# Relative and causal attention of a post-norm transformer kernel: the loops over steps written out on every engine

## The chip, the cores and the metric

One core of one Trainium2 chip runs the whole program, all nine stages in one launch. The metric is device time in microseconds (us) of one execution. The engines have their own instruction streams and meet at semaphores: TensorE (PE; PEld is its weight load), VectorE (DVE), ScalarE (ACT), GpSimd (POOL) and SyncE (SP, which issues most DMAs).

## The reference

The input is x of 8 batches x 512 tokens x 128 features. Four blocks follow one another, each with a residual and a layer norm: a one-head attention, a causal attention with 16 heads of 8 features together with a top-2-of-8 experts layer, an attention with relative positions, and a low-rank feed-forward. The change concerns two of the stages:

```python
# causal attention (16 heads of 8), b = 8, t = 512
scores = jnp.einsum('bqhd,bkhd->bhqk', q, k)
scores = jnp.where(mask, -jnp.inf, scores)
attn = jax.nn.softmax(scores / np.sqrt(HEAD_DIM), axis=-1)
ctx = jnp.einsum('bhqk,bkhd->bqhd', attn, v).reshape(b, t, EMB)
...
# relative attention (16 heads of 8)
AC = jnp.einsum('bhid,bhjd->bhij', q + u_bias[None, :, None, :], k)
BD = jnp.einsum('bhid,hjd->bhij', q + v_bias[None, :, None, :], rp)
BD = _rel_shift(BD)
attn = jax.nn.softmax((AC + BD) * scale, axis=-1)
out = jnp.einsum('bhij,bhjd->bhid', attn, v)
```

## The kernel before

Nothing is left to a scheduler: each phase writes out by hand what every engine does, in which order, and which semaphore count it waits for. Names of tiles in the profile begin with the phase's letter: `c_` for `phase_causal`, `r_` for `phase_relative`.

Both attention phases cut their work into NI = 32 steps: a step is one group of 4 heads (G = 4, NG = 4 groups) of one batch (NB = 8).

Causal, a step n: PE makes the row scores (L757, and the mask from `halves`, L765) three steps ahead in `ps_rows`, DVE takes their maxima (L917, L923), PE turns the maxima (L776), DVE splits them (L937, L939), and SP copies them beside the queries (L701). PE makes the scores of the step itself the other way round in `ps_keys` (L786), ACT takes the exponential (L860), POOL clears what lies above the diagonal (L891), PE sums probabilities and values (L798) in `ps_out`, ACT copies that to `osb` (L867; once a step) and SP stores it (L722). POOL issues the loads of step n + 5 (L691, L694).

Relative, a step n is 16 tiles u (four heads, four blocks of 128 queries each). For each tile PE makes one content matmul two tiles ahead in `ps_ac` (L1955), turns the finished scores of this tile in `ps_keys` (four transposes, L1962), and writes one bank of position scores of step n + 2 in `ps_wide` (short matmuls on 32 rows of weights, L1946, 192 in a step); after every fourth tile it sums a head in `ps_out` (L1973). DVE adds content and position and takes the maximum (L2078) and subtracts it (L2086). ACT takes the exponential (L2044), copies each bank to `wide` (L2023), and sends `wide`, 2,224 KB for half a step, to HBM (L2028); SP fetches it back skewed, 2,048 KB (L1866), which is the shift of the reference. SP also loads queries, keys and values (L1852, L1854, L1859) and stores the sums (L1894). ACT copies `ps_out` to `osb` once a step (L2034).

What the change touches is `steps` in each of the two phases (L704 and L1834): it calls an engine's `step` for every n. In the causal phase a loop on the engine (`Fori`, L705) runs 3 times over a body of 8 steps, and the last 8 are written out. In the relative phase the first 4 steps are written out, a loop (L1838) runs 6 times over a body of 4 steps, and the last 4 are written out. In a loop's body the count `it` is a register: waits compare a semaphore with a value worked out in registers, and DMAs take their places in HBM from registers. In the steps written out all of these are constants. `left` tells a step how many steps follow it, as far as it needs to know.

Each engine calls `steps` after its own preparation, so each of them has a loop of its own (POOL only in the causal phase).

Of the kernel before, what the change touches and what calls it, by code (L numbers as in the profile page):

```python
# [14 lines left out]
NB = 8  # L15
# [6 lines left out]
NI = NB * NG  # L22
# [18 lines left out]
class Chain:  # L41
# [6 lines left out]
    def step(self, ins):  # L48
        self.k += 1
        ins.then_inc(self.sem, 1)  # L50
        self.eng.wait_ge(self.sem, self.n * self.per + self.k)
# [563 lines left out]
def phase_causal(nc, sems, qk_stacks, v9_in, mask_in, ident_in, ctx_out):  # L615
# [14 lines left out]
    SLOTS = 8  # L630
    AHEAD = 3
    FIRST = 5
    ROUNDS = NI // SLOTS
# [7 lines left out]
    with ExitStack() as ctx:  # L641
# [60 lines left out]
                        .then_inc(m_loaded[s], 16)  # L702

        def steps(step, eng):  # L704
            with eng.Fori(0, ROUNDS - 1) as it:  # L705
                for s in range(SLOTS):
                    step(it, s, SLOTS)
            for s in range(SLOTS):
                step(ROUNDS - 1, s, SLOTS - 1 - s)

        @block.sync
        def _(sp):
# [21 lines left out]
            for n in range(2):  # L734
                sp.wait_ge(m_split, n + 1)
                load_maxima(sp, n)
            steps(step, sp)
            for s in range(SLOTS):
                sp.wait_ge(loaded[s], LOADS * ROUNDS)
# [5 lines left out]
        def _(pe):  # L745
# [103 lines left out]
            for f in range(BANKS):  # L849
                key_tiles(0, 0, 0, f)  # L850
            steps(step, pe)

        @block.scalar
        def _(act):
            def exponentials(n, p, f):
                e, c = FILLS[f]
                width = sum(WIDTH[j] for j in KEYS[c])
                at = OFF[KEYS[c][0]]
                act.wait_ge(keys_ps, NF * (2 * n + p) + f + 1)
                act.activation(probs[:, p, e, at:at + width], ps_keys[f % BANKS][:, 0:width], ACT.Exp, scale=SCALE)\  # L860
                    .then_inc(exp_done, 1)

            def take(n, s, uses):

                act.wait_ge(pair_done, 2 * n + 4)
                act.wait_ge(stored[s % 2], STORES * (uses + 2))
                act.activation(osb[:, s % 2, :, :, :].rearrange("q p e i -> q (p e i)"), ps_out[:, :], ACT.Copy)\  # L867
                    .then_inc(out_sb, 1)

            def step(it, s, left):  # L870
                n = SLOTS * it + s
                for p in range(2):
                    act.wait_ge(pair_done, 2 * n + p + 1)
                    for f in range(NF):
                        exponentials(n, p, f)
                        if p == 0 and f == 1:
                            take(n - 1, s - 1, SLOTS // 2 * it + (s - 1) // 2)

            act.sem_inc(exp_done, BANKS)
            steps(step, act)  # L880
            take(NI - 1, SLOTS - 1, NI // 2 - 1)
# [890 lines left out]
def phase_relative(nc, sems, qu_stacks, qv_stacks, k_stacks, v9_in, r_stack, ident_in, skew_dram, ctx_out):  # L1772
# [9 lines left out]
    STEP = 4  # L1782
# [3 lines left out]
    with ExitStack() as ctx:  # L1786
# [46 lines left out]

        def steps(step, eng):  # L1834

            for j in range(STEP):
                step(0, j, j == 0, 4)
            with eng.Fori(1, NB - 1) as it:  # L1838
                for j in range(STEP):
                    step(it, j, False, 4)  # L1840
            for j in range(STEP):
                step(NB - 1, j, False, STEP - 1 - j)

        def uses(it, j):

# [3 lines left out]
        def _(sp):  # L1849
# [61 lines left out]
            sp.wait_ge(wide_ps, 4 * NBK)  # L1911
            load_queries(0, 3)
            steps(step, sp)
            store(NI - 1)
            for s in range(2):
# [9 lines left out]
        def _(pe):  # L1925
# [87 lines left out]
            content_tile(0, 0, 0)  # L2013
            content_tile(0, 0, 1)
            steps(step, pe)
            value_head(NI - 1, 1, G - 1)

        @block.scalar
        def _(act):
# [40 lines left out]
            for n in range(2):  # L2060
                for c in range(2):
                    for bk in range(NBK):
                        copy_wide(n, n, c, bk)
                    send(n, n, c)
            steps(step, act)
            take_sums(NI - 1)

# [136 lines left out]
```

## Time and profile before

| what | us |
| --- | --- |
| three timed runs | 2204.28, 2189.57, 2207.71 (median 2204.28) |
| the profiled execution's own time | 2203.24 |
| its span, first to last instruction | 2201.5 |
| around the span | 1.7 |
| causal phase, first to last copy at L867 | 322.2 to 622.1 |
| relative phase, first to last copy at L2034 | 1212.2 to 2074.7 |

Times in the profile are microseconds from the start of the span. PE's busy time comes from pipelined matmuls with modelled ends. PEclk is the share of TensorE's full clock that was granted. "issue" as what ended an idle time means that the profile shows nothing that the engine waited for. A sequencer's own instructions (branch, register arithmetic) carry a q behind the engine's name.

### The profile page before, as it was taken

To read this page: it belongs to the slowest core of one execution; us is meant where nothing else is said; L and a number is where in the kernel's file an instruction comes from. 1 tells how busy PE (TensorE), PEld (TensorE's weight loads), DVE (VectorE), ACT (ScalarE), POOL (GpSimd) and SP (SyncE) were. 2 spreads that over 40 slices of the span, in tenths; PEclk is the share of its full clock that TensorE was granted. 3 is DMA by queue.
4 is the path that set the end of the run, shared out by engine and by line. 5 is a ranking of instruction groups with operands and counts; after the bars stand their busy time and mean duration, and the time that the engine had idled before them with its cause. 6 is when DMAs were issued, how large, how long until landed. Compare 5 with 4: busy or idle time off the path is not lost. (4 is left out here: it accounts for less than half of the span.)

```text
span 2201.5 us, 53937 instructions
## 1 busy us (share of the span) xinstructions
PE 1600.2 (73%) x19079; PEld 991.7 (45%) x19079; DVE 1297.3 (59%) x3126; ACT 1055.4 (48%) x2028; POOL 343.9 (16%) x659
## 2 busy tenths in 40 slices
PE   5532447777754999996536998687879787899647
PEld 2211214444433666663223555454546454555423
DVE  4774277667635666764314766474657565667636
ACT  4332316656722333222325766465657565667333
POOL 2232325545441000001300000000000000000023
PEclk8766659989966999998757988797989898889869
DMA  1114722222144121212889999898999999899621
GB/s 38 43 40 140 236 58 63 60 55 62 38 131 155 65 84 53 105 54 81 267 226 332 373 344 345 296 342 284 348 338 341 351 323 352 274 346 350 193 83 57
DMA packets 190973, 425.29 MB, mean 193 GB/s; under 512 B 37328, under 2 KB 86384, under 8 KB 181328
## 3 DMA queue, kind: packets, MB, share of 16 engines
q1 hardware_dynamic: 167776, 242.57, 35.5%
q10 hardware_dynamic: 12240, 150.28, 16.8%
q0 software_dynamic: 10720, 29.11, 5.1%
q8 instruction: 170, 2.79, 0.5%
q14 instruction: 67, 0.55, 0.1%
HBM read 218.59 MB, written 203.03 MB: 192 GB/s over the span
## 5 line engine op out<-in xcount | busy, mean ns | idle before, releaser
L2078 DVE CUSTOM_DVE_ANT_0 r_shifted<-r_ps_ac,r_shifted 128x512 f32<-128x512 f32 x512 | 351.9, 687 | 343.5 <-PE r_ps_ac L1955 327.0
L2044 ACT ACTIVATE r_probs<-r_ps_keys 128x512 f32<-128x512 f32 x512 | 309.7, 605 | 275.0 <-PE r_ps_keys L1962 249.5
L2023 ACT ACTIVATE r_wide<-r_ps_wide 128x512 f32<-128x512 f32 (+1 forms) x576 | 329.8, 590 | 102.1 <-PE r_ps_wide L1946 101.2
L1962 PE MATMUL r_ps_keys<-r_ident,r_shifted 128*128 128x128 f32 x2048 | 334.1, 288 | 7.5 <-issue 5.5
L1962 PEld LDWEIGHTS r_ps_keys<-r_ident,r_shifted 128*128 128x128 f32 x2048 | 273.8, 149 | 56.4 <-issue 15.4
L1946 PE MATMUL r_ps_wide<-r_r,r_qv 48*32 48x96 bf16 (+12 forms) x6144 | 238.3, 257 | 77.3 <-issue 67.2
L2086 DVE TENSOR_SCALAR r_shifted<-r_shifted,r_mx 128x512 f32<-128x512 f32 x512 | 249.2, 487 | 18.3
L1955 PE MATMUL r_ps_ac<-r_k,r_qu 128*128 128x512 bf16 x512 | 211.7, 414 | 60.8 <-DMA r_v<-v 32.8
L860 ACT ACTIVATE c_probs<-c_ps_keys 128x512 f32<-128x512 f32 (+1 forms) x384 | 174.8, 530 | 154.6 <-PE c_ps_keys L786 154.5
L1946 PEld LDWEIGHTS r_ps_wide<-r_r,r_qv 48*32 48x32 bf16 x6144 | 103.6, 95 | 179.0 <-issue 177.1
L1422 ACT ACTIVATE e_silu<-e_ps_a 128x1024 f32<-128x1024 f32 x64 | 65.7, 1027 | 216.1 <-PE e_ps_a L1355 215.9
L1973 PE MATMUL r_ps_out<-r_probs,r_v 128*9 128x128 f32 x4096 | 150.0, 285 | 21.6 <-issue 20.9
L923 DVE TENSOR_REDUCE c_mx_off<-c_ps_rows 128x2 f32<-128x768 f32 (+2 forms) x192 | 120.8, 686 | 68.3 <-PE c_ps_rows L757 68.3
L1069 POOL MEMSET n_zeros<- 128x4 f32 x1 | 0.1, 101 | 967.0 <-POOLq L1786 967.0
L1495 DVE TENSOR_TENSOR e_gu<-e_silu,e_ps_b 128x1024 f32<-128x1024 f32 x64 | 78.2, 1221 | 93.8 <-PE e_ps_b L1355 93.8
L1355 PE MATMUL e_ps_a<-e_hT_half,e_w_half 128*128 128x512 f32 x384 | 125.7, 463 | 4.3 <-DVE e_w_half L1550 4.3
L1973 PEld LDWEIGHTS r_ps_out<-r_probs,r_v 128*9 128x9 f32 x4096 | 103.2, 93 | 49.8 <-issue 36.1
L891 POOL TENSOR_SCALAR_AFFINE_SELECT c_probs<-c_probs 128x256 f32<-128x256 f32 x256 | 98.0, 407 | 162.3 <-ACT c_probs L860 161.8
L1955 PEld LDWEIGHTS r_ps_ac<-r_k,r_qu 128*128 128x128 bf16 x512 | 49.4, 97 | 163.7 <-issue 129.2
L1370 PE MATMUL e_ps_o<-e_weighed,e_w 128*128 128x512 f32 x256 | 120.5, 594 | 0.0
L786 PE MATMUL c_ps_keys<-c_qk 50*128 50x512 bf16 (+3 forms) x512 | 95.8, 317 | 27.7 <-ACT c_probs L860 19.5
L757 PE MATMUL c_ps_rows<-c_qk 48*128 48x128 bf16 (+2 forms) x896 | 78.0, 261 | 50.9 <-DVE c_mx_off L923 41.6
(214 smaller groups left out, 2157.0 us busy)
## 6 DMA issues: line engine op xcount, KB each, us to landing
skew<-r_wide ACTq DMA_DIRECT2D x64, 2224.0 KB, 11.8
r_shifted<-skew SPq DMA_DIRECT2D x64, 2048.0 KB, 18.0
e_weight_all<-weights SPq DMA_DIRECT2D x8, 2048.0 KB, 7.4
c_qk<-qk_stacks POOLq DMA_DIRECT2D x64, 192.0 KB, 3.7
stack<-d_part SPq DMA_DIRECT2D x96, 128.0 KB, 2.7
qk_stacks<-b_part SPq DMA_DIRECT2D x48, 128.0 KB, 3.6
qk_stacks<-b_part POOLq DMA_DIRECT2D x48, 128.0 KB, 3.7
stack<-d_part POOLq DMA_DIRECT2D x48, 128.0 KB, 3.7
```

The costliest lines, as they stand in the source:

```text
L860: act.activation(probs[:, p, e, at:at + width], ps_keys[f % BANKS][:, 0:width], ACT.Exp, scale=SCALE)\
L923: last = dve.tensor_reduce(off[:, :, NT * p + b], ps[:, :, at:at + width], AX_X, ALU.max)
L1355: last = pe.matmul(ps[:, k, :], w[a][:, e, k * P:(k + 1) * P], hT_halves[b][:, s, :], start=(i == 0), stop=(i == 2))
L1370: last = pe.matmul(ps_o[s][:, :], w3[:, e, k * P:(k + 1) * P], weighed[:, e % 4, k, :], start=(e == 0 and k == 0), stop=(e == NE - 1 and k ...
L1946: last = pe.matmul(ps[Q * a:Q * a + Q, frm - lo:to - lo], qv[rows, h, q0 + one:q0 + one + Q], r[rows, g // 2, h, at:at + to - frm], start= ...
L1955: pe.matmul(ps_ac[u % 2][:, :], qu[:, s, h, b * P:(b + 1) * P], k[:, s, h, :], start=True, stop=True)\
L1962: last = pe.transpose(ps_keys[u % 2][:, j * P:(j + 1) * P], shifted[:, s, u, j * P:(j + 1) * P], ident[:, :])
L1973: last = pe.matmul(ps_out[Q * b:Q * b + VW, h * P:(h + 1) * P], v9[:, s, j, h * VW:(h + 1) * VW], probs[:, h % 2, j, b * P:(b + 1) * P], s ...
L2023: act.activation(wide[:, s, c, lo:hi], ps_wide[bk % BANKS][:, 0:hi - lo], ACT.Copy).then_inc(wide_sb, 1)
L2044: act.activation(probs[:, h % 2, :, b * P:(b + 1) * P], ps_keys[u % 2][:, :].rearrange("p (j i) -> p j i", j=NT), ACT.Exp, scale=SCALE).th ...
L2078: dve.tensor_tensor_reduce(out=shifted[:, s, u, :], in0=ps_ac[u % 2][:, :], in1=shifted[:, s, u, :], scale=1.0, scalar=LOWEST, op0=ALU.add ...
L2086: dve.tensor_scalar(shifted[:, s, u, :], shifted[:, s, u, :], mx[:, u:u + 1], None, ALU.subtract).then_inc(s_ready, 1)
```

## The change

Both `steps` become one loop in the program that writes the kernel, so each engine gets 32 steps one behind the other, with constants in every wait and every address, and with neither loop nor branch. `left` is cut at the largest value that a step looks for (8, and 4). What a step does and in which order is the same.

```diff
@@ phase_causal
         def steps(step, eng):
-            with eng.Fori(0, ROUNDS - 1) as it:
-                for s in range(SLOTS):
-                    step(it, s, SLOTS)
-            for s in range(SLOTS):
-                step(ROUNDS - 1, s, SLOTS - 1 - s)
+            for n in range(NI):
+                step(n // SLOTS, n % SLOTS, min(SLOTS, NI - 1 - n))
@@ phase_relative
         def steps(step, eng):
 
-            for j in range(STEP):
-                step(0, j, j == 0, 4)
-            with eng.Fori(1, NB - 1) as it:
-                for j in range(STEP):
-                    step(it, j, False, 4)
-            for j in range(STEP):
-                step(NB - 1, j, False, STEP - 1 - j)
+            for n in range(NI):
+                step(n // STEP, n % STEP, n == 0, min(4, NI - 1 - n))
```

On PE in the causal phase, the end of the loop's body before (ISA and REGISTER_ALU are register work; the branch goes back to the first keys matmul of the next 8 steps):

```order
L786 MATMUL c_ps_keys<-c_qk 128x512
L783 REGISTER_ALU
L786 MATMUL c_ps_keys<-c_qk 128x384
L786 MATMUL c_ps_keys<-c_qk 128x128
L832 ISA
L798 MATMUL c_ps_out<-c_probs,c_v 9x128 x20
L705 REGISTER_ALU
L705 COMPARE_AND_BRANCH
```

On PE in the causal phase, the same place now (L795 is the old L798, L783 the old L786, L754 the old L757):

```order
L783 MATMUL c_ps_keys<-c_qk 128x512 x2
L783 MATMUL c_ps_keys<-c_qk 128x384
L783 MATMUL c_ps_keys<-c_qk 128x128
L795 MATMUL c_ps_out<-c_probs,c_v 9x128 x20
L783 MATMUL c_ps_keys<-c_qk 128x384
L783 MATMUL c_ps_keys<-c_qk 128x128
L754 MATMUL c_ps_rows<-c_qk 128x384 x2
```

The branch and the register work between the matmuls are gone; the matmuls stand in the same order.

On PE in the relative phase, the end of the loop's body and, behind the branch, what follows it:

```order
L1946 MATMUL r_ps_wide<-r_r,r_qv 32x224
L1946 MATMUL r_ps_wide<-r_r,r_qv 32x32
L1838 REGISTER_ALU
L1838 COMPARE_AND_BRANCH
L1955 MATMUL r_ps_ac<-r_k,r_qu 128x512
L1962 MATMUL r_ps_keys<-r_ident,r_shifted 128x128 x4
```

On PE in the relative phase, the first tile of the loop's body before:

```order
L1838 ISA
L1955 MATMUL r_ps_ac<-r_k,r_qu 128x512
L1959 REGISTER_ALU
L1962 MATMUL r_ps_keys<-r_ident,r_shifted 128x128 x4
L1991 ISA
L1931 ISA
L1946 MATMUL r_ps_wide<-r_r,r_qv 32x32
```

On PE in the relative phase, a tile now (L1947 is the old L1955, L1954 the old L1962, L1938 the old L1946, L1965 the old L1973):

```order
L1965 MATMUL r_ps_out<-r_probs,r_v 9x128 x16
L1947 MATMUL r_ps_ac<-r_k,r_qu 128x512
L1954 MATMUL r_ps_keys<-r_ident,r_shifted 128x128 x4
L1938 MATMUL r_ps_wide<-r_r,r_qv 32x160
L1938 MATMUL r_ps_wide<-r_r,r_qv 32x128
```

No matmul changed its place; what stood between them for the registers is gone on every engine.

## Rows read from the trace of the kernel before

**Rows 1.** The page: span, PE's busy share, DMA busy in 40 slices.
```profile
span 2201.5 us, 53937 instructions
PE 1600.2 (73%) x19079; PEld 991.7 (45%) x19079; DVE 1297.3 (59%) x3126; ACT 1055.4 (48%) x2028; POOL 343.9 (16%) x659
DMA  1114722222144121212889999898999999899621
```

**Rows 2.** The copies that mark a step (duration ns min/median/max, first and last start).
```profile
L867 ACT ACTIVATE c_osb<-c_ps_out x33: 597/597/603, 322.2 to 622.1; 128x512 f32<-128x512 f32 x33
...
L2034 ACT ACTIVATE r_osb<-r_ps_out x32: 591/603/604, 1212.2 to 2074.7; 128x512 f32<-128x512 f32 x32
```

**Rows 3.** Causal windows: length, busy us of PE, PEld, DVE, ACT, POOL; PEclk, DMA share, GB/s.
```profile
394.00:408.70 14.70, 8.96 (x137) 5.45 (x139) 6.68 (x11) 6.12 (x13) 5.05 (x12) 0.77 0.18 41
408.70:460.80 52.10, 40.77 (x802) 25.57 (x800) 40.10 (x66) 35.63 (x78) 29.84 (x67) 1.00 0.27 65
469.60:497.40 27.80, 20.92 (x268) 11.52 (x270) 13.45 (x22) 12.15 (x27) 9.99 (x23) 0.63 0.18 42
533.60:585.90 52.30, 40.76 (x800) 25.76 (x798) 40.11 (x66) 35.65 (x79) 27.79 (x64) 1.00 0.25 56
```

**Rows 4.** Relative windows, same columns; steps between copies: 3, 3, 4, 4, 4, 21.
```profile
1212.20:1289.20 77.00, 71.06 (x1202) 45.38 (x1201) 54.46 (x145) 54.83 (x107) 0.00 (x0) 0.93 1.03 357
1289.20:1371.70 82.50, 73.83 (x1205) 46.76 (x1208) 54.50 (x145) 55.22 (x107) 0.00 (x0) 0.90 1.00 354
1415.20:1534.60 119.40, 95.78 (x1605) 61.13 (x1604) 72.83 (x193) 73.19 (x142) 0.00 (x0) 0.89 0.92 321
1647.80:1760.20 112.40, 94.20 (x1604) 60.42 (x1603) 72.60 (x194) 73.08 (x142) 0.00 (x0) 0.91 0.96 341
1879.90:1988.20 108.30, 97.21 (x1602) 61.73 (x1600) 72.65 (x194) 73.12 (x142) 0.00 (x0) 0.89 0.97 333
...
1371.70:1988.20 616.50, 505.21 (x8401) 321.92 (x8400) 381.32 (x1009) 383.90 (x737) 0.00 (x0) 0.88 0.94 328
```

**Rows 5.** The loops' branches (duration ns min/median/max, first and last start).
```profile
L1838 PEldq COMPARE_BRANCH  x6: 76/5835/6406, 1395.9 to 1981.8; - x6
...
L705 PEldq COMPARE_BRANCH  x3: 79/4432/4572, 393.1 to 550.2; - x3
...
L1838 DVEq COMPARE_BRANCH  x6: 55/63/68, 1386.1 to 1972.3; - x6
```

**Rows 6.** PE's timeline behind the first and the fifth jump back, relative phase.
```profile
1402.45 0.61 PE L1955 MATMUL r_ps_ac<-r_k,r_qu 128*128 128x512 bf16 x1 [5.82 <-issue]
...
1408.47 0.63 PE L1946 MATMUL r_ps_wide<-r_r,r_qv 48*32 48x32 bf16 x8 [4.56 <-issue]
...
1867.96 0.61 PE L1955 MATMUL r_ps_ac<-r_k,r_qu 128*128 128x512 bf16 x1 [5.67 <-issue]
...
1873.71 0.62 PE L1946 MATMUL r_ps_wide<-r_r,r_qv 48*32 48x32 bf16 x8 [4.29 <-issue]
```

**Rows 7.** Windows around the first jump back, columns as in rows 3.
```profile
1395.00:1407.50 12.50, 3.09 (x29) 1.91 (x27) 2.37 (x6) 2.17 (x5) 0.00 (x0) 0.50 1.02 382
1407.50:1420.00 12.50, 11.53 (x171) 7.02 (x172) 6.43 (x17) 6.68 (x13) 0.00 (x0) 0.74 0.34 68
```

**Rows 8.** DMA between 1371.7 and 1988.2: all packets, and the instruction queue's packets.
```profile
DMA packets 72714, 201.98 MB, mean 328 GB/s; under 512 B 14206, under 2 KB 21304, under 8 KB 67273
...
q8 instruction: 83, 1.36, 0.9%
```

**Rows 9.** PE's register arithmetic for two waits (duration ns min/median/max).
```profile
L1931 PEldq ALU_OP  x384: 32/32/36, 1285.0 to 1980.3; - x192
...
L783 PEldq ALU_OP  x237: 32/32/36, 322.2 to 549.0; - x119
```

**Rows 10.** PE's timeline: two idle times away from a branch, relative phase.
```profile
1228.86 0.61 PE L1973 MATMUL r_ps_out<-r_probs,r_v 128*9 128x128 f32 x11 [1.70 <-issue]
...
1452.85 0.28 PE L1946 MATMUL r_ps_wide<-r_r,r_qv 48*32 48x256 bf16 x1 [2.28 <-issue]
```

## The prediction

> **What bounds the kernel now.** I read the page first, for the stages in which the two loops run: PE is busy 73% of the 2201.5 us span, and the DMA engines stand at 8 or 9 tenths in the second half, where the relative phase lies [rows 1]. Then I looked for a mark that comes once a step, and took ACT's copy of the sums: 33 in the causal phase, 32 in the relative one [rows 2]. Cutting the trace at these copies shows the pace.
>
> In the causal phase six steps take 52.1 us, 8.7 us each, with the clock at full and no engine above 80%: PE, DVE and ACT hand work to each other (40.8, 40.1 and 35.6 us busy of 52.1). After eight and after sixteen steps, where the loop jumps back, the pace breaks: the step at 394.0 takes 14.7 us, the two at 469.6 take 27.8 us [rows 3].
>
> In the relative phase the six steps 1212.2 to 1371.7 take 77.0 + 82.5 = 159.5 us, 26.6 each, with DMA at its limit (share 1.00 to 1.03, 354 to 357 GB/s). Of these, three are written out and three lie in the loop's first pass, and no jump back lies between. Four steps of the last pass, again without one, take 108.3 us. Four steps with one jump back take 119.4 us, at best 112.4. Over the 21 steps from 1371.7 to 1988.2, which hold all five jumps back, the pace is 616.5 / 21 = 29.4 us, and the DMA share sinks to 0.94 [rows 4]. So this phase is bound by the DMA round trip of the wide scores, except behind a jump, where PE holds everybody up.
>
> The branch rows say whose jump it is. PE's compare-and-branch takes 76 ns once in the relative phase (the exit, which falls through) and up to 6406 ns otherwise, median 5835; in the causal phase 79 ns once, and 4432 and 4572 ns. DVE's takes 55 to 68 ns [rows 5]. PE's timeline has the cost in two parts: 5.82 us idle before the first content matmul of the new pass, then one tile, then 4.56 us idle before the first wide matmul, both ended by "issue", at the first jump; 5.67 and 4.29 us at the fifth [rows 6]. 
>
> Two jumps back in the causal phase go. The step at 394.0 falls from 14.7 to 8.7 us, the two at 469.6 from 27.8 to 2 x 8.7 = 17.4: 6.0 + 10.4 = 16.4 us. The branches alone are 4.57 + 4.43 = 9.0 of that. The rest is what follows: the granted clock is 0.77 and 0.63 in these windows and 1.00 in the steady ones, so part of the matmuls there ran at 1.2 instead of 2.4 GHz behind PE's idle time [rows 3, 5]. What is late next is the old round of PE, DVE and ACT at 8.7 us. Bounds for the term: 9 and 16.4; I take 16.4, since the windows on either side of the jumps keep to 8.7.
>
> Five jumps back in the relative phase go. Counted at PE they are 5 x (5.75 + 4.4) = 51 us, with the means of the first and the fifth [rows 6]. But PE is not alone on the path, so I count by pace as well. While PE stood at the first jump, the DMA engines still worked off what was queued (share 1.02, 382 GB/s from 1395.0 to 1407.5) and ran dry only then (0.34, 68 GB/s in the next 12.5 us) [rows 7]: PE's stall becomes a hole in the DMA stream, a little later and about as long, 0.66 x 12.5 = 8.3 us. Ten steps without a jump take 159.5 + 108.3 = 267.8 us, 26.8 each; 21 such steps take 562.4 us instead of 616.5. That is 54.1 us, and the term that I take. What is late next is the DMA traffic. It bounds the gain: 201.98 MB in these 21 steps [rows 8] at 382 GB/s need 529 us, so no more than 87 us. From below, four steps keep 108.3 us of their last pass, 27.1 each: 616.5 - 569 = 47 us.
>
> The register arithmetic goes, at 32 ns each on PE: 384 for the wide banks alone, 237 for the key tiles [rows 9]. I put it at nothing. The cover is in the trace: six looped causal steps take 52.1 us and six written-out ones 52.3 [rows 3]. In the relative phase the DMA engines cover it. If that cover were thin, 384 x 32 ns = 12 us is the end on the side of a gain; none is on the side of a loss, as nothing is added in its place.
>
> The DMAs' addresses become constants on SP and POOL. Their queues run ahead of the data and the bytes are the same, so I put this at nothing too, bounded by the same two causal windows, in which SP stores and POOL loads with registers in one and constants in the other.
>
> The loops' set-up and the exits (76 and 79 ns on PE) are worth less than 1 us together.
>
> Code grows, which costs if it has to be fetched more often. PE's was fetched all along: the instruction queue moved 83 packets in these 21 steps [rows 8], four a step, so a pass of four steps was loaded anew each time. The number stays or falls. Crossing into a new piece of code can show: PE idles 2.28 us before the wide matmul at 1452.85 inside the loop, and 1.70 us at 1228.86 in steps already written out, both with "issue" [rows 10]. Such idle times are in the 26.8 us already.
>
> The sum: 2203.24 - 16.4 - 54.1 - 0 = 2132.7 us, against the profiled execution, which lies 1.0 under the median of 2204.28. I predict 2132.
>
> At the branch two pages can be weighed against the rows. The Trainium skill, "Advanced Engine Details and Errata", section Control Flow Timing, gives a compare-and-branch about 108 ns; by that, an estimate from this page, the seven jumps back cost 0.8 us in all and the change would be worth nothing. The Trainium skill, "Runtime: NRT & Kernel Launch", section Instruction fetch mechanics, says that a taken branch to code outside the two blocks at hand has to wait for a DMA fetch. This trace sides with the second for PE (4.4 to 6.4 us) and with the first for DVE (63 ns).
>
> **The rivals.**
>
> *The transfers hide it.* The relative phase hangs on DMA, so PE's stalls only move waiting from one place to another, and the pace stays 29.4 us. Only the causal 16.4 us are left: 2187. For it speaks the DMA share of 0.94 over the 21 steps. Against it speak the hole of 0.34 behind the jump and the windows at 26.6 and 27.1 us.
>
> *The pace goes down to the wire.* The holes left in the jump-free windows are echoes of the jumps and the start, and the phase closes up to 382 GB/s: 2203.2 - 16.4 - 87 = 2100. Against it: the first six steps, with no jump before them, had 26.6 us, and 529 / 21 would be 25.2.
>
> *A branch costs nothing; PE stood for another reason* that the rows don't name, and the time is the old one less 1 us: 2202. Against it: all seven long branches stand where a jump is taken, and both exits take under 0.1 us.
>
> *Code fetch takes the branch's place (slower).* Written out, every piece of PE's code is new, and pieces may begin at places where PE has little queued. There are 83 - 5 = 78 such crossings in the 21 steps. Two or three a pass show now, at some 2.3 us [rows 10]. From 70.5 / 2.3 = 31 more of them on the nothing is won; if the 65 or so that are hidden all showed, it is 65 x 2.3 = 150 us lost, and 2283 us. Against it: the steps 1212.2 to 1289.2, written out, kept 25.7 us each, and six written-out causal steps kept 8.7. A milder case, 15 more that show, gives 2132 + 35 = 2167, still faster.
>
> **How the numbers follow.** Chances: the forecast 0.78 (own range 2110 to 2147: 21 steps at 25.7 us, the fastest jump-free window of rows 4, or at 27.5, the slowest); down to the wire 0.08; transfers hide it 0.06; milder code fetch 0.02; branch costs nothing 0.02; code fetch slower 0.04. Range: from the wire, 2100, less the 12 us of register work at half, so 2094, up to the milder fetch with room, 2172. A measurement of this kernel tells about 1% from no change. Faster by over 1% (under 2182): 0.78 + 0.08 + 0.02 = 0.88. Within 1%: 0.06 + 0.02 = 0.08. Slower: 0.04.
>
> **What would show it.** Right: no branch rows of PE in either phase; the copies of the sums 8.7 us apart throughout the causal phase; PE without the pairs of 5 to 6 and 4 to 5 us "issue" in the relative phase; its 21 steps at 26 to 27.5 us with the DMA share at 1.0 and the granted clock above 0.90. Wrong: more "issue" idle times of 2 to 3 us on PE than two or three in four steps (code fetch); or PE idle without "issue", behind DVE or a load, and the pace near 29 (transfers). The prediction fails if the relative steps stay above 28.5 us, or if the causal saving is under 9 us.

## The result and the profile after

| | before | changed |
| --- | --- | --- |
| timed runs, median us | 2196.93 of 4 | 2139.12 of 4 (2134.5 to 2144.5) |
| the profiled execution's own time | 2203.24 | 2137.47 |
| its span | 2201.5 | 2135.9 |
| causal phase, first to last copy of the sums | 299.9 | 282.3 |
| between the phases, last causal to first relative copy | 590.1 | 595.2 |
| relative phase, first to last copy | 862.5 | 809.8 |

The ratio of the changed kernel to the one before is 0.9726, 95% interval 0.9685 to 0.9766: 2.7% faster. Between the two medians lie 57.8 us, between the two profiled executions 65.7. A second comparison, at the end, gave 0.971 (0.9671 to 0.9749).

The page of the changed kernel, the lines that answer to [rows 1], and the granted clock:

```profile
span 2135.9 us, 49719 instructions
...
PE 1582.6 (74%) x19079; PEld 983.5 (46%) x19079; DVE 1296.6 (61%) x3126; ACT 1054.0 (49%) x2028; POOL 342.4 (16%) x659
...
PEclk8765759999966999998855999899899999989869
DMA  1113822222144121121889999999999999999522
```

Every engine does the same work. 4,218 recorded instructions are gone, all of the sequencers. DMA stands at 9 tenths from the start of the relative phase nearly to its end, where it had dips before.

The windows of the changed kernel, cut at the same copies as [rows 3] and [rows 4] (columns: from:to, length, busy us of PE, PEld, DVE, ACT, POOL; PEclk, DMA share, GB/s):

```profile
393.70:402.40 8.70, 6.76 (x135) 4.31 (x133) 6.68 (x11) 5.94 (x13) 4.90 (x12) 1.00 0.29 65
402.40:454.80 52.40, 40.73 (x800) 25.84 (x798) 40.06 (x66) 35.66 (x79) 29.61 (x67) 1.00 0.27 66
463.50:480.90 17.40, 13.51 (x268) 8.59 (x266) 13.35 (x22) 11.87 (x26) 9.75 (x23) 1.00 0.28 66
1199.70:1358.20 158.50, 143.96 (x2403) 91.97 (x2401) 109.00 (x289) 109.41 (x212) 0.00 (x0) 0.90 1.03 365
1358.20:1924.90 566.70, 502.27 (x8401) 319.27 (x8400) 381.01 (x1009) 383.71 (x736) 0.00 (x0) 0.92 1.01 353
```

The causal step at the old jump takes 8.7 us instead of 14.7, the two at the second jump 17.4 instead of 27.8, and the clock is granted in full there (1.00). The register work has left nothing behind: six steps take 52.4 us as they took 52.1. In the relative phase the 21 steps of [rows 4] take 566.7 us instead of 616.5, 27.0 each, at a DMA share of 1.01 instead of 0.94.

Who waited for whom in these 21 steps, changed kernel (waiting engine and line, who released it: us in total, times, the longest):

```profile
PEld r_ps_wide L1938 <- issue: 79.5, 347, 2.6
...
PEld r_ps_ac L1947 <- DMA r_v<-v: 24.9, 7, 5.3
...
PEld r_ps_out L1965 <- issue: 19.9, 29, 2.7
...
PE r_ps_wide L1938 <- issue: 13.5, 12, 1.9
```

And the kernel before, over its 21 steps:

```profile
PEld r_ps_ac L1955 <- issue: 103.3, 241, 6.1
PEld r_ps_wide L1946 <- issue: 102.2, 342, 5.2
PE r_ps_wide L1946 <- issue: 38.5, 16, 4.8
```

The long idle times that nothing explains are gone from these steps; what is left of them is at most 2.7 us (before the sums, L1965). PE's longest single waits are now for a load, the values of the next step (up to 5.3 us, seven times), which SP issues as it does the skewed fetches. The instruction queue moved 68 packets in these steps, where [rows 8] had 83:

```profile
q8 instruction: 68, 1.11, 0.8%
```

### The profile page after: what moved, and what is told of

Same layout as the page of the kernel before. It is cut to its first block and busy times, and to the rows that moved or that the text cites. A ratio compares the mean times of both kernels' runs of the same rounds, so it can differ in the third digit from the quotient of the medians.

```text
span 2135.9 us, 49719 instructions
## 1 busy us (share of the span) xinstructions
PE 1582.6 (74%) x19079; PEld 983.5 (46%) x19079; DVE 1296.6 (61%) x3126; ACT 1054.0 (49%) x2028; POOL 342.4 (16%) x659
## 3 DMA queue, kind: packets, MB, share of 16 engines
q10 hardware_dynamic: 12240, 150.28, 17.4%
## 5 line engine op out<-in xcount | busy, mean ns | idle before, releaser
L1954 PE MATMUL r_ps_keys<-r_ident,r_shifted 128*128 128x128 f32 x2048 | 333.9, 289 | 9.9 <-issue 5.9
L1954 PEld LDWEIGHTS r_ps_keys<-r_ident,r_shifted 128*128 128x128 f32 x2048 | 272.5, 149 | 56.7 <-issue 13.9
L1938 PE MATMUL r_ps_wide<-r_r,r_qv 48*32 48x96 bf16 (+12 forms) x6144 | 237.5, 258 | 42.1 <-issue 31.1
L1947 PE MATMUL r_ps_ac<-r_k,r_qu 128*128 128x512 bf16 x512 | 210.2, 411 | 47.8 <-DMA r_v<-v 33.2
L1419 ACT ACTIVATE e_silu<-e_ps_a 128x1024 f32<-128x1024 f32 x64 | 65.7, 1027 | 216.3 <-PE e_ps_a L1352 216.3
L1938 PEld LDWEIGHTS r_ps_wide<-r_r,r_qv 48*32 48x32 bf16 x6144 | 103.6, 95 | 144.1 <-issue 142.7
L1965 PE MATMUL r_ps_out<-r_probs,r_v 128*9 128x128 f32 x4096 | 149.7, 285 | 19.4 <-issue 18.7
L1965 PEld LDWEIGHTS r_ps_out<-r_probs,r_v 128*9 128x9 f32 x4096 | 103.0, 93 | 46.6 <-issue 28.4
L1947 PEld LDWEIGHTS r_ps_ac<-r_k,r_qu 128*128 128x128 bf16 x512 | 49.3, 97 | 153.6 <-issue 76.4
L754 PE MATMUL c_ps_rows<-c_qk 48*128 48x128 bf16 (+2 forms) x896 | 75.1, 253 | 53.0 <-DVE c_mx_off L920 43.9
L783 PE MATMUL c_ps_keys<-c_qk 50*128 50x512 bf16 (+3 forms) x512 | 91.9, 309 | 20.1 <-ACT c_probs L857 19.9
```

Of the source, the lines that this page charges most:

```text
L1938: last = pe.matmul(ps[Q * a:Q * a + Q, frm - lo:to - lo], qv[rows, h, q0 + one:q0 + one + Q], r[rows, g // 2, h, at:at + to - frm], start= ...
L1947: pe.matmul(ps_ac[u % 2][:, :], qu[:, s, h, b * P:(b + 1) * P], k[:, s, h, :], start=True, stop=True)\
L1954: last = pe.transpose(ps_keys[u % 2][:, j * P:(j + 1) * P], shifted[:, s, u, j * P:(j + 1) * P], ident[:, :])
L1965: last = pe.matmul(ps_out[Q * b:Q * b + VW, h * P:(h + 1) * P], v9[:, s, j, h * VW:(h + 1) * VW], probs[:, h % 2, j, b * P:(b + 1) * P], s ...
```

## The experiments

The copies of the sums cut every trace in the same way. All causal and relative lengths below are from first to last copy, of one profiled execution each; times and ratios are of rounds against the kernel before on the same chip.

| run | causal us | between | relative us | jumps back, causal / relative | median us | ratio |
| --- | --- | --- | --- | --- | --- | --- |
| before | 299.9 | 590.1 | 862.5 | 2 / 5 | | |
| before again | 290.6 | 593.1 | 869.4 | 2 / 5 | 2204.56 | 1.0013 |
| changed | 282.3 | 595.2 | 809.8 | 0 / 0 | 2139.12 | 0.9726 |
| changed again | 281.8 | 598.3 | 809.3 | 0 / 0 | 2140.8 | 0.971 |
| causal only | 281.2 | 594.5 | 823.2 | 0 / 5 | 2157.32 | 0.9818 |
| relative only | 294.6 | 593.3 | 814.9 | 2 / 0 | 2156.9 | 0.9809 |
| PE only | 282.5 | 597.0 | 822.6 | 0 / 0 on PE | 2153.95 | 0.9779 |
| all but PE | 293.0 | 592.5 | 850.8 | 2 / 5 on PE | 2188.24 | 0.9946 |
| twelve steps | 294.7 | 591.4 | 826.3 | 2 / 1 | 2163.88 | 0.9832 |
| six steps | 308.7 | 594.2 | 844.4 | 3 / 5 | 2197.89 | 0.9994 |
| moved by 40 | 295.2 | 593.0 | 834.9 | 2 / 5 | 2177.94 | 0.989 |
| moved by 128 | 294.3 | 604.5 | 838.3 | 2 / 5 | 2192.29 | 0.997 |
| moved by 256 | 297.1 | 627.1 | 847.5 | 2 / 5 | 2224.03 | 1.0103 |
| changed, moved by 128 | 282.3 | 604.7 | 812.8 | 0 / 0 | 2146.0 | 0.9746 |

**One phase at a time.**

```diff
# phase_causal (first run) or phase_relative (second run) as in the change, the other phase as before
-            with eng.Fori(...) as it:
...
+            for n in range(NI):
```

Expected of the causal phase alone:

> Only the causal phase's loop is written out; the relative phase keeps its loop. Theory (PE's jumps back cost their own time and a stretch at the low clock): the 33 copies of the causal sums stand 8.7 us apart with no break, the causal phase ends 17 to 18 us earlier than in the kernel before, and the whole kernel is 14 to 19 us shorter (ratio 0.992 to 0.994). Rival (the gain of the whole change lies in the relative phase alone, the causal phase only moved its waiting): less than 5 us shorter.

Expected of the relative phase alone:

> Only the relative phase's loop is written out. Theory: the 21 steps between the seventh and the twenty-eighth copy of the relative sums fall from 616.5 to 562 to 570 us, no idle time of PE of 5 us and more with issue behind it at the old places, and the kernel is 43 to 55 us shorter (ratio 0.975 to 0.981). Together with the causal one alone this sums to the whole change. Rival (the transfers hide PE's jumps): under 15 us shorter.

Measured: 0.9818 (0.9768 to 0.9867) and 0.9809 (0.9769 to 0.985). The relative phase alone gives 44 us, within the 43 to 55 expected; its phase takes 814.9 us instead of 862.5. The causal phase alone gives 44 us, over twice what its theory allows. Its own part is as expected (281.2 us), but the untouched relative phase fell to 823.2 us, with its five long jumps still there:

```profile
L1835 PEldq COMPARE_BRANCH  x6: 83/5766/6542, 1381.9 to 1926.8; - x6
```

The two gains add up to 88 us, more than the change gives. So something in the relative phase's loss is not the jump: it went when code ahead of it changed its length. PE's timeline of this run behind the third jump shows one thing that is different:

```profile
1608.70 0.61 PE L1952 MATMUL r_ps_ac<-r_k,r_qu 128*128 128x512 bf16 x1 [5.89 <-issue]
1609.10 1.06 PE L1959 MATMUL r_ps_keys<-r_ident,r_shifted 128*128 128x128 f32 x4
1610.09 0.63 PE L1943 MATMUL r_ps_wide<-r_r,r_qv 48*32 48x32 bf16 x8
```

The first idle time of [rows 6] is there, 5.89 us, and the second is missing, here and behind the four other jumps: the wide matmuls follow without a pause.

**Where the code lies.** To test that, PE's code was moved without touching the loops.

```diff
# moved by 40: in phase_relative, PE, before it waits for its constants
+            for _ in range(40):
+                pe.sem_inc(bank_marks, 1)
# moved by 128 and by 256: in phase_experts, PE, before it waits for its constants
+            for _ in range(128):
+                pe.sem_inc(pads, 1)
```

> The kernel before, with 40 semaphore increments (nobody waits for them) at the start of PE's relative phase, where PE waits for its loads anyway: all of PE's code behind is moved by 40 instructions. Theory (the second idle time of 4.0 to 4.8 us after each jump is the next piece of code, which begins some 20 instructions behind the jump's target): with the target moved past that border the second idle time goes at all five jumps, and the kernel is 10 to 22 us shorter. Rival (the second idle time has to do with the start of a pass, with its first wide bank): it stays at all five, and the time is within 5 us of before.

> The kernel before with 256 semaphore increments on PE at the start of the experts phase, where PE waits for its loads anyway: PE's code behind is moved by 256 instructions, which is 16384 bytes at 64 bytes each, the size of one packet of the instruction queue. Theory (code is fetched in pieces of 16384 bytes, and the second idle time comes where a piece ends some 20 instructions behind the jump's target): the borders fall where they fell before, so the pairs of idle times are back at all five jumps and the time is that of before within 0.5%. Rival (any shift helps, or the 40 instructions of the run before acted in another way): the second idle time is gone and the kernel is 15 us or more shorter.

> The same with 128 increments, half a piece. Theory: the border lies some 150 instructions behind the jump's target, PE has queued work when it gets there, the second idle time is gone at all five jumps, and the kernel is 20 to 35 us shorter than before (ratio 0.984 to 0.991), still 15 to 30 us longer than the changed kernel, since the jumps themselves stay. Rival (the shift doesn't matter): within 5 us of before.

Moved by 40, the second idle time is gone behind all five jumps; these are the idle times behind the first and the fifth, each alone:

```profile
1405.48 0.61 PE L1955 MATMUL r_ps_ac<-r_k,r_qu 128*128 128x512 bf16 x1 [6.23 <-issue]
...
1847.70 0.61 PE L1955 MATMUL r_ps_ac<-r_k,r_qu 128*128 128x512 bf16 x1 [4.27 <-issue]
```

The relative phase falls to 834.9 us, and the kernel is 1.1% faster (0.9826 to 0.9955) for 40 instructions more, some 23 us where 10 to 22 were expected. Moved by 256, the pairs are back behind all five jumps; the first and the fifth:

```profile
1430.67 0.60 PE L1958 MATMUL r_ps_ac<-r_k,r_qu 128*128 128x512 bf16 x1 [5.30 <-issue]
1437.24 0.62 PE L1949 MATMUL r_ps_wide<-r_r,r_qv 48*32 48x32 bf16 x8 [5.11 <-issue]
...
1896.13 0.61 PE L1958 MATMUL r_ps_ac<-r_k,r_qu 128*128 128x512 bf16 x1 [5.58 <-issue]
1901.87 0.62 PE L1949 MATMUL r_ps_wide<-r_r,r_qv 48*32 48x32 bf16 x8 [4.29 <-issue]
```

Moved by 128, they are gone again and the relative phase takes 838.3 us. So the second idle time is a border between two pieces of code, 256 instructions apart, that lay just behind the jump's target.

The instruction queue's own packets say the same. Every packet of it in these traces holds 16384 bytes. Between the end of the first jump of the kernel before (1402.3) and 1406.0 the queue has no packet; then it has one, which starts at 1406.05 and takes 1.10 us (the DMA view of 1406.0 to 1408.4: packets, MB, share):

```profile
q8 instruction: 1, 0.02, 2.9%
```

PE's wide matmuls follow at 1408.47. So it goes behind all five jumps of the kernel before, of its repeat and of the kernel moved by 256: the next packet starts 3.2 to 4.6 us after the branch has ended, and PE starts again 1.2 to 1.5 us after it has landed. Moved by 40, the packet comes as late (3.4 to 4.2 us after the branch), but PE doesn't need it yet. The long branches themselves end 1.2 to 1.6 us after a packet has landed, in both phases of the kernel before and of its repeat; no packet lands within any of their short ones.

The runs with another causal phase fit too. PE's instructions ahead of the relative loop can be counted in a trace, a loop's body once. Causal only has some 4170 more than the kernel before, about 70 beyond a multiple of 256, and no second idle time. Six steps, below, has about 580 fewer: its border lies about 80 instructions behind the target instead of 16, and PE's weight load stands idle there for 1.5 to 2.4 us instead of 4.3 to 5.6. Behind its first jump:

```profile
1412.09 1.39 PEld L1973 LDWEIGHTS r_ps_out<-r_probs,r_v 128*9 128x9 f32 x28 [2.38 <-issue]
```

The times of the last two runs came out wrong against what was expected, 1.0103 and 0.997 instead of 1.00 and 0.984 to 0.991, and the table says why: the increments themselves were dear. Between the phases the run moved by 256 lost 34 to 37 us. PE's timeline at the start of the experts phase shows 50.07 us of idle time, where the kernel before had 16.36:

```profile
714.73 1.08 PE L1333 MATMUL e_ps_t<-e_ident,e_z 128*128 128x128 f32 x4 [50.07 <-issue]
```

The expectation was that PE's wait for its loads would cover them.

**The number of jumps, and a shorter body.**

```diff
# twelve steps: phase_relative, body three times as long
-            with eng.Fori(1, NB - 1) as it:
-                for j in range(STEP):
-                    step(it, j, False, 4)
+            with eng.Fori(0, 2) as half:
+                for i in range(3):
+                    for j in range(STEP):
+                        step(3 * half + i + 1, j, False, 4)
# six steps: phase_causal, SLOTS = 6 (so six buffers instead of eight), 4 passes, then 8 steps
# written out; SP's last waits count accordingly
-            with eng.Fori(0, ROUNDS - 1) as it:
+            with eng.Fori(0, 4) as it:
...
-            for s in range(SLOTS):
-                step(ROUNDS - 1, s, SLOTS - 1 - s)
+            for n in range(4 * SLOTS, NI):
+                step(n // SLOTS, n % SLOTS, min(SLOTS, NI - 1 - n))
```

> The kernel before with the relative loop's body three times as long (12 steps, 2 passes): one jump back instead of five; the causal phase as before. Theory (a price of some 10 us for each jump back): 4 x 10 = 40 us shorter, 33 to 45, and one long branch of PE left in that phase. Rival (it is not the number of jumps, but registers and loop as such): under 15 us shorter.

> The causal phase with six slots and a loop's body of 6 steps (some 1730 PE instructions instead of 2310), 4 passes and so 3 jumps back instead of 2, then 8 steps written out; the relative phase as before. Theory (a jump is dear only when its target is no longer held by PE; a body of 616 instructions elsewhere in this kernel jumps in 231 ns, one of 2310 in 4.4 us): if 1730 instructions are still held, the three branches take under 0.3 us each and the causal phase is 16 to 18 us shorter. Rival (any jump of this phase costs its 4.4 us and what follows): three breaks of 6 to 10 us instead of two, the kernel 5 to 10 us longer than before.

With one jump instead of five the relative phase takes 826.3 us, 36 us less, and the kernel is 1.7% faster (0.9768 to 0.9896). Registers and loop stayed, so it is the jumps and what comes right behind them; the pair of idle times is still there at the one that is left. The shorter body was a miss for the theory: its 1735 PE instructions (counted in the trace between two branches) are not held either.

```profile
L705 PEldq COMPARE_BRANCH  x4: 76/4573/4917, 372.5 to 555.2; - x4
```

All three jumps take 4.6 to 4.9 us, the causal phase gets longer (308.7 us, 8.9 for each jump over the 282.0 without any; the six buffers may have a share in that), and this is the rival's case. The kernel as a whole took the time of before (0.9994), not 5 to 10 us more, since the relative phase behind it was shorter (844.4 us) with its border moved. The body that does jump cheaply is the experts phase's, 616 instructions, in the kernel before:

```profile
L1240 PEldq COMPARE_BRANCH  x2: 76/154/231, 857.0 to 935.9; - x2
```

Between 616 and 1735 lies the size up to which PE finds the jump's target at hand; no run narrows it down. What the jump costs beyond its own time can be read in this run too, in the windows of the step around the first jump and of its second half. The step takes 17.8 us instead of 8.7. In its second half the clock was granted at 0.50, and PE was busy for 8.46 of 9.00 us.

```profile
373.40:391.20 17.80, 12.12 (x135) 6.51 (x137) 6.77 (x11) 6.19 (x13) 5.21 (x12) 0.58 0.15 34
382.20:391.20 9.00, 8.46 (x109) 4.50 (x103) 3.97 (x8) 3.42 (x8) 2.40 (x6) 0.50 0.19 44
```

**Which engine's loop.**

```diff
# PE only: both phases
-            with eng.Fori(...) as it:
+            if eng is nc.tensor:
+                for n in range(NI):
...
+            else:
+                with eng.Fori(...) as it:
# all but PE: the same with "is not"
```

> Both loops are written out on PE alone; ACT, DVE, SP and POOL keep loops and register arithmetic. Theory (only PE's jump is dear): as fast as the changed kernel within 5 us, 2134 to 2146. Rival (the other engines' loops, their register arithmetic or their DMA addresses from registers carry part of the gain): over 2155.

> Both loops are written out on ACT, DVE, SP and POOL; PE alone keeps its loops. Theory (only PE's jump is dear): as slow as the kernel before within 5 us, with PE's seven long branches of 4.4 to 6.4 us still there. Rival (the other engines' loops carry part of the gain): 10 us or more shorter than the kernel before.

PE alone gives 0.9779 (0.9748 to 0.981), 47 us; all but PE give 0.9946 (0.9916 to 0.9976), 12 us. Both medians lie outside what the theory "only PE's jump is dear" said: 2154 instead of 2134 to 2146, and 12 us instead of at most 5. They fit each other: about four fifths are PE's, and some 12 us come from writing out the other engines' loops. The traces show them in the relative phase, 822.6 us with PE alone against 809.3 and 809.8, and 850.8 with all but PE against 862.5 and 869.4. But they are not a slower pace in the loop: with PE alone the 21 steps of [rows 4] take 565.2 us, against 566.7 and 567.2 in the changed kernel, and the extra lies in the six steps before and the four behind. Which engine and which of its instructions carry them wasn't tried and stays open.

**The changed kernel moved, and both kernels again.**

> The changed kernel, with 128 such increments at the same place: PE's written-out code is moved by 128 instructions against the borders of the pieces in which it is fetched. If where the borders fall matters (the slower rival of the prediction), the time moves by over 10 us one way or the other; if PE's queue and the transfers mostly hide the crossings, it stays within 5 us of the changed kernel, with other places of 1.2 to 3.5 us idle behind issue.

> The kernel before, unchanged, for a second profile. Every theory expects the time of before (ratio 1.00 within 0.5%) and the same pairs of idle times behind all five jumps of the relative phase (5.1 to 6.4 and 4.0 to 4.8 us). What it is for: how far a phase's length moves between two executions. The causal phase of before lasted 299.8 us from first to last copy, four other kernels with the same loop 293 to 295; I expect 295 here, and the relative phase within 8 us of 862.5.

> The changed kernel, unchanged, for a second profile beside these. Every theory expects its time (ratio 0.970 to 0.977), the causal phase at 282 to 283 us from first to last copy and the relative one within 6 us of 809.8. It sets how much of the 15 us by which the kernel with PE alone written out lies above it is more than the scatter.

Written-out code hardly minds where the borders fall, by this one shift: moved by 128, the relative phase takes 812.8 us instead of 809.8. The kernel's median, 2146.0 us, is 5 to 7 us above the changed kernel's, a little more than the 5 of the expectation, as the increments delayed the phase's start (604.7 us between the phases instead of 595.2 and 598.3). The repeats show what scatter a single profile has: the causal phase of the kernel before took 299.9 and then 290.6 us, its relative phase 862.5 and then 869.4; the changed kernel's phases moved by 0.5 us each. Windows of the kernel before, again, over both phases:

```profile
322.00:612.60 290.60, 221.23 (x4130) 136.37 (x4126) 193.55 (x320) 189.25 (x415) 149.66 (x337) 0.96 0.23 55
1205.70:2075.10 869.40, 703.11 (x11785) 469.77 (x11962) 556.48 (x1474) 547.76 (x1044) 0.00 (x0) 0.88 0.93 325
```

## Why the prediction was right

**The sum.** 70.5 us were forecast between the two profiled executions, 65.7 came (2203.24 to 2137.47), and 62 between the second pair's spans (2201.8 to 2139.4). The measured 2139 lies 7 us above the predicted 2132 and within the forecast's own range. The medians differ by less, 57.8 us in the first comparison and 60.0 in the last (2200.81 to 2140.8): the forecast was 10 to 13 us too large against these.

**The causal term**, 16.4 us: 17.6 in the first pair of profiles, but it was sized from an unlucky trace. The seven other runs in the table with two jumps took 290.6 to 297.1 us, mean 294.2; the five without took 281.2 to 282.5. The usual price is 12 us, 6 for each jump, of which the branch itself is about 4. That the number came out in the first pair is luck: against the usual price the term was 4 us too large. The part put on the lower clock is borne out by the shorter body: behind its first jump the clock was granted at 0.50 in the second half of a step. How much of the price it is was not measured apart.

**The relative term**, 54.1 us: 49.8 in the 21 steps, 52.7 over the whole phase, 56 between the means of both pairs (866.0 to 809.6). The pace without jumps was forecast at 26.8 us and measured at 27.0, at a DMA share of 1.01. Taking it from windows without a jump was the step that held; so did the limit, as nothing ran to the wire's 25.2.

**The account of that term was half right.** The prediction counted 5.75 + 4.4 us at each jump and read both as instructions that had not arrived, which the packets of the instruction queue bear out. But it read both as the jump's, to go only with it, and the runs that moved the code part them: the second idle time belongs to the place of the code behind the jump. The 21 steps that hold the five jumps give its size (windows of causal only, moved by 40, moved by 256, moved by 128):

```profile
1363.80:1932.20 568.40, 492.05 (x8402) 317.52 (x8400) 381.52 (x1009) 382.58 (x736) 0.00 (x0) 0.93 0.99 348
1376.70:1958.70 582.00, 481.45 (x8275) 321.74 (x8400) 381.79 (x1009) 384.39 (x737) 0.00 (x0) 0.91 0.99 343
1406.60:2008.80 602.20, 481.29 (x8275) 321.70 (x8400) 380.97 (x1009) 383.53 (x737) 0.00 (x0) 0.88 0.95 332
1382.70:1970.70 588.00, 485.36 (x8276) 322.53 (x8400) 381.70 (x1009) 385.67 (x736) 0.00 (x0) 0.90 0.97 339
```

With all jumps and without the second idle time they take 568.4, 582.0 and 588.0 us; with it 616.5 and 625.7 (the kernel before) and 602.2 (moved by 256). So it carried 14 to 57 us, 35 between the means. The jumps themselves, with good placement, carry 1 to 21 us over the changed kernel's 567, 13 in the mean or under 3 each, less than the 5.8 us for which PE stands, which fits the DMA engines working on in the meantime, as [rows 7] show for the first jump. These are single profiles, and they scatter: moved by 256 has all five pairs back and is still 14 to 24 us shorter here than the kernel before. That the second idle time goes and comes with the place of the code is shown; its size in the whole is rough.

**The register arithmetic and constant addresses**, put at nothing: held in the causal phase (52.4 us for six steps as before). Writing out the other engines' loops brought some 12 us, which the sum put at nothing. That the prediction had named 12 us as the end of its range for PE's register arithmetic is a coincidence: these are other engines, and the 12 us are not shown to be register work.

**Outside the sum.** Between the two phases, where no line changed, the changed kernel lost 5 us in both pairs (595.2 and 598.3 against 590.1 and 593.1). The other runs that add nothing ahead of the relative phase lie between 591 and 597 whatever is written out, so a small loss is likely and its cause open.

**The rivals.** "The transfers hide it" fell: with DMA at 1.01 the pace is 27.0, not 29.4. "A branch costs nothing" fell with the twelve-step body. "Down to the wire" did not come. The slower rival, crossings that begin to show in written-out code, did not come: what PE idles there for no reason shown is 2.7 us at most in the 21 steps. But it named the right kind of cost, for the kernel before: a crossing at a bad place behind the jump cost about as much as the jump or more.

## What to carry to other kernels

A hardware loop is cheap while its body fits what the engine keeps of its code (616 instructions jumped in 0.23 us) and dear on TensorE when it doesn't (3.5 to 7.3 us for 1735 and more): look at the duration of the taken branch in the trace before anything else, and write out, or lengthen the body of, the loops in which it is long. Two idle times in a row with no releaser behind a jump are two different things; moving the code by some tens of instructions tells them apart, and won 1% by itself here. Where the transfers are the limit, take the gain from the pace in windows without the disturbance, not from the stalls counted at one engine.

## What was not expected of the hardware

Code comes to PE in pieces of 256 instructions: moved by 40 or 128 instructions the second idle time vanished behind all five jumps, moved by 256 it was back, and each packet of PE's instruction queue holds 16384 bytes. A border 16 instructions behind a jump's target (one content matmul and four transposes, each with its weight load, and six of the sequencer) costs 3.9 to 5.2 us of PE's idle time (4.3 to 5.6 us of its weight load's), one about 80 instructions behind it 1.5 to 2.4 us of the weight load's. The reason is in the packets: the piece that follows the target's starts to move only 3.2 to 4.6 us after the branch has ended, and PE has run through what it has by then. Why it isn't asked for sooner isn't shown. Away from a jump, PE's unexplained idle times last at most 2.7 us in the 21 steps of the changed kernel, and once 3.1 us near the end of the phase in its repeat.

Semaphore increments on PE that are written one behind the other are not free: 256 of them lengthened PE's idle time before its first matmul of the experts phase by 33.7 us (50.07 instead of 16.36). In the traces they start 0.15 us apart, in the rows of 128 as in that of 256, while a single one is recorded with 51 ns.
